# Attention and mixture feed-forward layer on 8 cores: slot waits kept across query halves, and the next head's operand copies issued one head earlier

## The chip, the cores and the metric

The program runs on all 8 cores of one Trainium2 chip. Every core works on two of the 16 sequences, with the same instructions, and no core talks to another. The metric is the device time of the slowest core in microseconds. The clock that is spoken of below is the one that TensorE (PE) was granted in a stretch, as a share of 2.4 GHz: 1.00 is 2.4 GHz and 0.50 is 1.2 GHz.

## What is computed

`x` is 16 x 2048 x 1024. After a layer norm the layer computes an attention with two steps, in which the output of step 0 is the query of step 1, and a feed-forward network with low-rank experts, of which each token uses two. Their product is added to `x`. The part around the change is the loop over steps:

```python
q = _l2norm(q)
k = _l2norm(k)
state = q
for _ in range(STEPS):                      # STEPS = 2
    sim = jnp.einsum('bqhd,bkhd->bqhk', state, k)
    att = jax.nn.softmax(BETA * sim, axis=-1)
    state = jnp.einsum('bqhk,bkhd->bqhd', att, v)
o = state.reshape(B, S, H) @ Wo + bo        # 16 heads of 64, S = 2048
...
x = x + s * silu(ffn(xn))
```

## The kernel before

Each core runs its two sequences one after the other. For each: norm and transposes; the projections to q, k and v (kept in SBUF as `qbuf`, `kbuf`, `vbuf`, bf16); the attention loop; the output projection; the feed-forward network over two halves of the tokens. A fence of all engines stands between these stages.

**The order of work is written out by hand.** A helper, `Prog.op`, appends an instruction to its engine's stream, in program order, with waits on counters: `tc_` counts TensorE instructions that release something, `vc` VectorE (DVE), `sc` ScalarE (ACT). A wait such as `(sc, sc.v)` is for the value that the counter has been brought to at the moment of writing, so it is for everything that was written before it on that engine. Every DVE and ACT instruction also waits for the one before it on its own engine. Each engine works through its stream in order.

**The attention loop** runs over 2 steps, 16 heads (`hh`) and 2 halves of the queries (`qh`, 1024 queries each). One pass through the inner body is called a half here. There are 64 halves per sequence, 128 per core. In a half, the 2048 keys are worked through in 16 chunks `c` of 128:

- `emit_sim(c)` (L613): two matmuls of 128x512 write the similarities of chunk `c` to half `c % 2` of `psb`. The first waits for the head's operands (`head_in`) and for the slot of `psb` (`sim_rel`).
- L629: ACT takes the exponential of 128x1024 from `psb` to the buffer `att[c % 4]` ("exp" below).
- L635: two matmuls add `v` times that into `psa`, over all 16 chunks. The first of a half also waits for `acc_gate`.
- `emit_sim` runs two chunks ahead of L635. At the start of a half chunks 0 and 1 are written first.

**The end of a half**: DVE copies the sum out of `psa` (L646, 65 rows, the last of them the softmax denominator), and ACT makes the reciprocal of that row by Ln (L649) and Exp (L652).

**The boundary between two heads** has two more parts. `head_copies(hh, step)` prepares the operands of a head in `kaugs[z]` and `staugs[z]`, with `z = hh % 2`: two DVE copies (L549, L552). In step 1 it also does ACT Square (L555), four pairs of a matmul (L559) and an ACT Ln (L563), an ACT Exp of the whole row (L567) and a DVE scaling (L569). `flush_tail` normalises the head before last: four times a pair of a 1-row fp32 matmul (two PE instructions, L586) and a DVE copy (L591), each waiting for the other, and after every second pair a DVE multiply into `qbuf` (L594). Its matmuls wait for `vc` at the value of the moment of writing.

So at the end of head `hh` the order of writing is: L646, L649, L652 of its second half, `head_copies(hh + 1)`, `flush_tail(hh - 1)`, and then the first half of head `hh + 1`. At the end of head 0 there is no tail to flush. After head 15 the last two tails are flushed.

At the start of each half, before, the lists of releases are written anew: `sim_rel` and `att_rel` with the values that `sc` and `tc_` have at that moment, `acc_gate` with that of `vc`. The last value of `sc` written by then is that of L652 (or of L567 after it), and that of `vc` belongs to L646, to L569 or to the last L594.

Of the kernel before, what the change touches and what calls it, by code (L numbers as in the profile page):

```python
# [18 lines left out]
NHEAD = 16  # L19
# [131 lines left out]
def build_program(S=2048, NB=2, dedup=True):  # L151
# [72 lines left out]
    tc_ = p.ctr("tc")  # L224
    vc = p.ctr("vc")
    sc = p.ctr("sc")
# [30 lines left out]
    def SC(fn, waits=(), inc=None, incn=1):  # L257
        p.op("scalar", fn, waits, inc, incn)
# [27 lines left out]
    for b in range(NB):  # L286
# [16 lines left out]
        for i in range(n_tt):  # L303
            sl = i % 2
            Y(lambda e, sl=sl, i=i, b=b: e.dma_start(out=xt[sl], in_=x_h[b, 128 * i:128 * (i + 1), :]),
              waits=[xrel[sl]], inc=xld[sl], incn=16)
            ldw = (xld[sl], xld[sl].v)
            SC(lambda e, sl=sl: e.activation(sqf, xt[sl], AF.Square),
               waits=[ldw, (vc, vc.v)], inc=sc)
            V(lambda e, sl=sl, i=i: e.reduce_sum(statc[:, i:i + 1], xt[sl], axis=AX.X),  # L310
              waits=[ldw], inc=vc)
            V(lambda e, i=i: e.reduce_sum(statc[:, 16 + i:17 + i], sqf, axis=AX.X),
              waits=[(sc, sc.v)], inc=vc)
# [30 lines left out]
        for i in range(n_tt):  # L344
            sl = i % 2
            Y(lambda e, sl=sl, i=i, b=b: e.dma_start(out=xt[sl], in_=x_h[b, 128 * i:128 * (i + 1), :]),
              waits=[xrelA[sl]], inc=xld[sl], incn=16)
# [3 lines left out]
              waits=[ldw, stats_done, (tc_, tc_.v)], inc=vc)  # L351
# [60 lines left out]
        for i in range(n_tt):  # L412
# [3 lines left out]
          waits=[(tc_, tc_.v)], inc=vc)  # L416
# [155 lines left out]
            return (vc, vc.v)  # L572

        tail_rel = [(vc, 0)]
        for step in range(2):
            heads_ready = [None] * (NHEAD + 1)
            heads_ready[0] = head_copies(0, step)
# [21 lines left out]
            for hh in range(NHEAD):  # L599
                z = hh % 2  # L600
                kaug = kaugs[z]
                stin = staugs[z]
                head_in = heads_ready[hh]
                for qh in range(NQH):
                    qco = HL * qh
                    sim_rel = [[(sc, sc.v)], [(sc, sc.v)]]
                    att_rel = [[(tc_, tc_.v)] for _ in range(4)]
                    acc_gate = [(vc, vc.v)]

                    def emit_sim(c):  # L610
                        sb = c % 2
                        for j2 in range(HL // 512):
                            T(lambda e, c=c, sb=sb, j2=j2, qco=qco, stin=stin, kaug=kaug: e.matmul(  # L613
                                psb[:, 1024 * sb + 512 * j2:1024 * sb + 512 * (j2 + 1)],
                                kaug[0:128, 128 * c:128 * (c + 1)],
                                stin[0:128, qco + 512 * j2:qco + 512 * (j2 + 1)],
                                start=True, stop=True),
                              waits=([head_in] + sim_rel[sb]) if j2 == 0 else [],
                              inc=(tc_ if j2 == HL // 512 - 1 else None))
                        return tc_.v  # L620

                    simv = [0] * n_tt
                    simv[0] = emit_sim(0)
                    if n_tt > 1:
                        simv[1] = emit_sim(1)
                    for c in range(n_tt):
                        sb = c % 2
                        ab = c % 4
                        SC(lambda e, ab=ab, sb=sb: e.activation(att[ab], psb[:, 1024 * sb:1024 * sb + HL],  # L629
                                                                AF.Exp),  # L630
                           waits=[(tc_, simv[c])] + att_rel[ab], inc=sc)
                        scv = sc.v
                        sim_rel[sb] = [(sc, scv)]
                        for j2 in range(HL // 512):
                            T(lambda e, c=c, ab=ab, j2=j2, hh=hh: e.matmul(  # L635
                                psa[0:128, 512 * j2:512 * (j2 + 1)],
                                vbuf[:, 1040 * c + 65 * hh:1040 * c + 65 * hh + 128],
                                att[ab][:, 512 * j2:512 * (j2 + 1)],
                                start=(c == 0), stop=(c == n_tt - 1)),
                              waits=([(sc, scv)] + (acc_gate if c == 0 else [])) if j2 == 0 else [],  # L640
                              inc=(tc_ if (c == n_tt - 1 and j2 == HL // 512 - 1) else None))
                        att_rel[ab] = [(tc_, tc_.v)]
                        if c + 2 < n_tt:
                            simv[c + 2] = emit_sim(c + 2)
                    st_ready = tc_.v
                    V(lambda e, z=z, qco=qco: e.tensor_copy(  # L646
                        stg[z][:, qco:qco + HL], psa[0:65, 0:HL]),
                      waits=[(tc_, st_ready)])
                    SC(lambda e, z=z, qco=qco: e.activation(  # L649
                        stg[z][64:65, qco:qco + HL], stg[z][64:65, qco:qco + HL], AF.Ln),  # L650
                       waits=[(vc, vc.v), (tc_, tc_.v)], inc=sc)
                    SC(lambda e, z=z, qco=qco: e.activation(  # L652
                        stg[z][64:65, qco:qco + HL], stg[z][64:65, qco:qco + HL],
                        AF.Exp, scale=-1.0), inc=sc)
                stg_v = (vc.v, sc.v)
                heads_ready[hh + 1] = head_copies(hh + 1, step) if hh + 1 < NHEAD else None
                if pending_tail is not None:
                    flush_tail(pending_tail)
                pending_tail = (hh, z, stg_v)
# [431 lines left out]
```

How the kernel before makes its waits and increments, by code:

```python
        def run(engine, _w=wlist, _inc=inc, _incn=incn, _fn=fn, _eng=eng):  # L68
            seen = self._waited[_eng]
            for c, v in _w:
                if self.dedup and seen.get(c.name, 0) >= v:
                    continue
                engine.wait_ge(c.sem, v)
                seen[c.name] = v
            inst = _fn(engine)
            if _inc is not None:
                inst.then_inc(_inc.sem, _incn)
            return inst
```

## Time and profile before

| | us |
|---|---|
| median of 2 runs | 12471.17 |
| lowest, highest | 12468.47, 12473.87 |
| the profiled execution | 12428.32 |
| its span, slowest core (core 6) | 12426.8 |
| spans of the eight cores | 12349.3 to 12426.8 |

The rows below come from the slowest core of the profiled execution. Times are microseconds from its first instruction. In a timeline a row is a run of like instructions of an engine: start, time it takes, engine, line, operation, tiles and count, and in brackets how long the engine had been idle before it and which instruction ended that.

### The profile page before, as it was taken

What the parts mean: (1) busy time and instruction counts of PE and PEld (TensorE: products, weight loads), DVE (VectorE), ACT (ScalarE), POOL (GpSimd) and SP (SyncE); (2) the same over time, 40 slices, a digit from 0 to 9 for tenths busy, and PEclk for the clock granted to TensorE, in tenths of its full rate; (3) what the DMA queues carried; (4) which work ended last, traced back from release to release, by engine and by line L of the source; (5) the groups of instructions that cost most, each with busy time, mean ns of one, the idle gap of its engine ahead of it and who ended that gap; (6) DMA issues with size and microseconds to landing.
All of it is one profiled execution on the core that took longest, in us unless ns stands there. A gap on an engine that the chain in (4) does not pass through costs nothing.

```text
span 12426.8 us, 89949 instructions; the slowest of 8 cores (12349.3 to 12426.8 us)
## 1 busy us (share of the span) xinstructions
PE 8045.1 (65%) x28266; PEld 2834.9 (23%) x28800; DVE 3310.3 (27%) x5351; ACT 3262.3 (26%) x3764; POOL 70.7 (1%) x137
## 2 busy tenths in 40 slices
PE   3566776666557773777446667766664687738775
PEld 2221111111123331333122211111111233313331
DVE  5222111111133332333352221111111333323333
ACT  1114665655200000000011146565661000000000
POOL 0000000000000000000000000000000000000000
PEclk6667887777778885889656678877777788858886
DMA  3100000000211102111120000000002011011111
GB/s 88 23 8 1 0 1 0 0 0 0 59 32 25 28 18 59 25 28 29 56 86 8 8 0 0 1 0 0 0 0 79 12 29 23 18 59 23 29 23 47
DMA packets 77408, 287.73 MB, mean 23 GB/s; under 512 B 8826, under 2 KB 17172, under 8 KB 66708
## 3 DMA queue, kind: packets, MB, share of 16 engines
q0 software_dynamic: 19040, 130.84, 5.6%
q1 hardware_dynamic: 57908, 151.10, 3.7%
q8 instruction: 246, 4.03, 0.1%
q14 instruction: 214, 1.75, 0.0%
HBM read 354.03 MB, written 58.72 MB: 33 GB/s over the span
## 4 chain that ended last, share of the span: by engine, by line
PE 49%; ACT 20%; DVE 17%; issue 8%; DMA 4%; SPq 1%; DVEq 1%; ACTq 1%; POOLq 0%
ACT arena L629 15%; PE psa L852 7%; PE psb L852 7%; PE psa L905 6%; PE psb L905 4%; PE psa L586 4%; PE psa L635 2%; PE psb L613 2%; DMA arena<-x 2%; PE psb L887 2%; PE psa L486 1%; DVE arena L876 1%; DVE arena L895 1%; DVE arena L591 1%; DVE arena L920 1%
## 5 line engine op out<-in xcount | busy, mean ns | idle before, releaser
L629 ACT ACTIVATE arena<-psb 128x1024 bf16<-128x1024 f32 x2048 | 2095.1, 1023 | 1291.7 <-PE psb L613 1041.0
L635 PE MATMUL psa<-arena 128*128 128x512 bf16 x4032 | 1296.7, 403 | 417.7 <-ACT arena L629 182.5
L613 PE MATMUL psb<-arena 128*128 128x512 bf16 x3986 | 1348.7, 428 | 325.5 <-ACT arena L652 254.5
L852 PE MATMUL psa<-arena 128*128 128x512 bf16 x4012 | 989.2, 388 | 131.6 <-DVE arena L920 111.7
L852 PE MATMUL psb<-arena 128*128 128x512 bf16 x4012 | 986.5, 387 | 4.7
L871 ACT ACTIVATE arena<-psa 128x512 f32<-128x512 f32 x256 | 152.8, 597 | 3155.6 <-PE psa L859 3143.6
L646 DVE COPY arena<-psa 65x1024 f32<-65x1024 f32 x128 | 156.3, 1221 | 2812.3 <-PE psa L635 2812.3
L905 PE MATMUL psa<-arena 128*128 128x512 bf16 x2008 | 741.7, 546 | 128.8 <-DVE arena L895 122.6
L586 PE MATMUL psa<-arena,onescf 1*64 1x512 f32 x512 | 484.3, 1046 | 467.0 <-DVE arena L594 153.5
L613 PEld LDWEIGHTS psb<-arena 128*128 128x128 bf16 x4096 | 419.5, 105 | 1001.2 <-issue 627.9
L905 PE MATMUL psb<-arena 128*128 128x512 bf16 x2008 | 534.7, 423 | 125.2 <-DVE arena L895 122.4
L635 PEld LDWEIGHTS psa<-arena 128*128 128x128 bf16 x4096 | 290.1, 100 | 1422.7 <-issue 1419.2
L852 PEld LDWEIGHTS psa<-arena 128*128 128x128 bf16 x4096 | 398.0, 99 | 662.1 <-issue 278.2
L887 PE MATMUL psb<-arena 128*128 128x512 bf16 x504 | 183.5, 450 | 527.2 <-DVE arena L881 404.2
L852 PEld LDWEIGHTS psb<-arena 128*128 128x128 bf16 x4096 | 407.1, 99 | 504.4 <-issue 90.4
L876 DVE TENSOR_TENSOR arena<-psa,arena 128x512 f32<-128x512 f32 x256 | 177.1, 692 | 1083.8 <-PE psa L859 1070.6
L920 DVE TENSOR_TENSOR arena<-psa,arena 128x512 f32<-128x512 f32 x480 | 332.1, 692 | 485.2 <-PE psa L905 484.8
L920 DVE TENSOR_TENSOR arena<-psb,arena 128x512 f32<-128x512 f32 x480 | 332.1, 692 | 289.8 <-PE psb L905 289.4
L905 PEld LDWEIGHTS psa<-arena 128*128 128x128 bf16 x2048 | 261.3, 132 | 639.2 <-issue 600.0
L871 ACT ACTIVATE arena<-psb 128x512 f32<-128x512 f32 x256 | 152.8, 597 | 867.8 <-PE psb L859 855.8
L876 DVE TENSOR_TENSOR arena<-psb,arena 128x512 f32<-128x512 f32 x256 | 177.1, 692 | 668.8 <-PE psb L859 655.5
L990 PE MATMUL psb<-idents,arena 128*128 128x128 f32 x256 | 114.4, 447 | 360.2 <-DVE arena L993 249.1
(165 smaller groups left out, 6276.9 us busy)
## 6 DMA issues: line engine op xcount, KB each, us to landing
arena<-wfs POOLq DMA_DIRECT2D x64, 1728.0 KB, 11.7
arena<-x SPq DMA_DIRECT2D x96, 512.0 KB, 3.7
xnsp<-arena SPq DMA_DIRECT2D x64, 256.0 KB, 3.9
arena<-xnsp SPq DMA_DIRECT2D x16, 1024.0 KB, 7.1
ssp<-arena SPq DMA_DIRECT2D x64, 256.0 KB, 2.6
arena<-ssp SPq DMA_DIRECT2D x32, 512.0 KB, 4.5
out<-arena SPq DMA_DIRECT2D x32, 512.0 KB, 2.9
nxsp<-arena SPq DMA_DIRECT2D x64, 128.0 KB, 4.3
```

What stands on the lines that cost most here:

```text
L486: T(lambda e, c=c, qsl=qsl, cols=cols, sl=sl: e.matmul(bankA(qsl), wsl[0][sl][:, 128 * c:128 * (c + 1)], x2T[:, S * c + cols.start:S * c + ...
L586: T(lambda e, z2=z2, qco2=qco2, j2=j2: e.matmul(psa[0:64, 1024:1536], onescf[64:65, :], stg[z2][64:65, qco2 + 512 * j2:qco2 + 512 * (j2 + 1)],
L613: T(lambda e, c=c, sb=sb, j2=j2, qco=qco, stin=stin, kaug=kaug: e.matmul(psb[:, 1024 * sb + 512 * j2:1024 * sb + 512 * (j2 + 1)], kaug[0:1 ...
L629: SC(lambda e, ab=ab, sb=sb: e.activation(att[ab], psb[:, 1024 * sb:1024 * sb + HL], AF.Exp), waits=[(tc_, simv[c])] + att_rel[ab], inc=sc)
L635: T(lambda e, c=c, ab=ab, j2=j2, hh=hh: e.matmul(psa[0:128, 512 * j2:512 * (j2 + 1)], vbuf[:, 1040 * c + 65 * hh:1040 * c + 65 * hh + 128] ...
L646: V(lambda e, z=z, qco=qco: e.tensor_copy(stg[z][:, qco:qco + HL], psa[0:65, 0:HL]), waits=[(tc_, st_ready)])
L852: wslb=wslb, tco=tco: e.matmul(grp(bank_i), wslb[:, FC * c + 128 * m:FC * c + 128 * (m + 1)], nxh[:, TH * c + tco:TH * c + tco + TC], star ...
L871: SC(lambda e, bi=bi, grp=grp: e.activation(silu_s[:, 512 * bi:512 * (bi + 1)], grp(bi), AF.Silu), waits=[(tc_, h1v), (vc, vc.v)], inc=sc)
L876: V(lambda e, bi=bi, grp=grp, j=j, tco=tco: e.tensor_tensor(h3w_s[:, 512 * bi:512 * (bi + 1)], grp(KC + bi), wexp[j][:, tco:tco + TC], ALU ...
L887: T(lambda e, c4=c4, j=j, rbank=rbank, sl=sl: e.matmul(rbank, a2sl[sl][:, 128 * c4:128 * (c4 + 1)], act2w[j][:, TC * c4:TC * (c4 + 1)], st ...
L905: sl=sl: e.matmul(grp(dd4), wsl2[sl][:, D * c4 + 128 * dd:D * c4 + 128 * (dd + 1)], act2w[j][:, TC * c4:TC * (c4 + 1)], start=(j == 0 and ...
L920: V(lambda e, dd=dd, dd4=dd4, grp=grp, tco=tco, wv=wv: e.tensor_tensor(outb[:, TH * dd + tco:TH * dd + tco + TC], grp(dd4), outb[:, TH * d ...
```

## The change

Two things are moved, and no instruction is added or taken away.

1. `sim_rel`, `att_rel` and `acc_gate` are set once ahead of both steps and then carried from half to half. The first similarities of a half wait for the exps that read the two slots of `psb` last, and no longer for L652. The first L635 of a half waits, for `psa`, for the L646 before it, and no longer for the last DVE instruction written.
2. `head_copies(hh + 1)` is written at the start of head `hh` rather than at its end. At a boundary between heads the order of writing is now: L646, L649, L652 of head `hh`, `flush_tail(hh - 1)`, `head_copies(hh + 2)`, first half of head `hh + 1`. Ahead of head 0 of each step stand `head_copies(0)` and `head_copies(1)`, and at the boundary from head 14 to 15 there are no copies.

```diff
         tail_rel = [(vc, 0)]
+        sim_rel = [[(sc, sc.v)], [(sc, sc.v)]]
+        att_rel = [[(tc_, tc_.v)] for _ in range(4)]
+        acc_gate = [[(vc, vc.v)]]
         for step in range(2):
...
                 head_in = heads_ready[hh]
+                if hh + 1 < NHEAD:
+                    heads_ready[hh + 1] = head_copies(hh + 1, step)
                 for qh in range(NQH):
                     qco = HL * qh
-                    sim_rel = [[(sc, sc.v)], [(sc, sc.v)]]
-                    att_rel = [[(tc_, tc_.v)] for _ in range(4)]
-                    acc_gate = [(vc, vc.v)]
...
-                              waits=([(sc, scv)] + (acc_gate if c == 0 else [])) if j2 == 0 else [],
+                              waits=([(sc, scv)] + (acc_gate[0] if c == 0 else [])) if j2 == 0 else [],
...
                       waits=[(tc_, st_ready)])
+                    acc_gate[0] = [(vc, vc.v)]
...
                 stg_v = (vc.v, sc.v)
-                heads_ready[hh + 1] = head_copies(hh + 1, step) if hh + 1 < NHEAD else None
                 if pending_tail is not None:
                     flush_tail(pending_tail)
```

## Rows read from the trace of the kernel before

**Rows 1.** The page: the chain that ended last, by line, and the costliest group.
```profile
ACT arena L629 15%; PE psa L852 7%; PE psb L852 7%; PE psa L905 6%; PE psb L905 4%; PE psa L586 4%; PE psa L635 2%; PE psb L613 2%; DMA arena<-x 2%; PE psb L887 2%; PE psa L486 1%; DVE arena L876 1%; DVE arena L895 1%; DVE arena L591 1%; DVE arena L920 1%
...
L629 ACT ACTIVATE arena<-psb 128x1024 bf16<-128x1024 f32 x2048 | 2095.1, 1023 | 1291.7 <-PE psb L613 1041.0
```

**Rows 2.** Windows: steps 0 and 1, first sequence; last three columns: clock, DMA share, GB/s.
```profile
1088.00:2060.00 972.00, 692.04 (x2125) 193.19 (x2168) 136.17 (x153) 591.11 (x576) 0.00 (x0) 0.82 0.00 0
2060.00:3245.00 1185.00, 747.45 (x2202) 201.41 (x2246) 158.98 (x181) 689.67 (x672) 0.00 (x0) 0.76 0.00 0
```

**Rows 3.** Timeline, ACT: from the first half to the second of head 0.
```profile
1098.47 11.55 ACT L629 ACTIVATE arena<-psb 128x1024 bf16<-128x1024 f32 x10
...
1113.38 1.05 ACT L652 ACTIVATE arena<-arena 1x1024 f32<-1x1024 f32 x1
1115.68 2.19 ACT L629 ACTIVATE arena<-psb 128x1024 bf16<-128x1024 f32 x2 [1.25 <-PE psb L613]
```

**Rows 4.** Timeline, PE: the same boundary.
```profile
1110.16 0.59 PE L635 MATMUL psa<-arena 128*128 128x512 bf16 x2 [0.58 <-ACT arena L629]
1114.57 1.86 PE L613 MATMUL psb<-arena 128*128 128x512 bf16 x4 [3.82 <-ACT arena L652]
1116.95 1.01 PE L635 MATMUL psa<-arena 128*128 128x512 bf16 x2 [0.52 <-ACT arena L629]
```

**Rows 5.** Windows over the same boundary; PE's clock is the third number from the end.
```profile
1110.00:1115.00 5.00, 1.02 (x4) 0.31 (x5) 1.22 (x1) 2.12 (x3) 0.00 (x0) 0.75 0.00 0
1115.00:1120.00 5.00, 4.47 (x12) 1.22 (x10) 0.00 (x0) 3.07 (x3) 0.00 (x0) 0.57 0.00 0
```

**Rows 6.** Timeline, step 0, boundary from head 1 to head 2.
```profile
1186.66 1.22 DVE L646 COPY arena<-psa 65x1024 f32<-65x1024 f32 x1 [24.42 <-PE psa L635]
...
1189.61 1.93 PE L586 MATMUL psa<-arena,onescf 1*64 1x512 f32 x2 [3.05 <-DVE arena L552]
...
1199.54 1.94 PE L586 MATMUL psa<-arena,onescf 1*64 1x512 f32 x2 [0.94 <-DVE arena L591]
...
1201.40 1.89 PE L613 MATMUL psb<-arena 128*128 128x512 bf16 x4
...
1202.53 2.19 ACT L629 ACTIVATE arena<-psb 128x1024 bf16<-128x1024 f32 x2 [12.31 <-PE psb L613]
```

**Rows 7.** Timeline, step 0, first matmul pair of the tail one head later.
```profile
1252.01 1.54 PE L586 MATMUL psa<-arena,onescf 1*64 1x512 f32 x2 [3.06 <-DVE arena L552]
```

**Rows 8.** Timeline, step 1, boundary from head 1 to head 2.
```profile
2196.61 1.22 DVE L646 COPY arena<-psa 65x1024 f32<-65x1024 f32 x1 [24.44 <-PE psa L635]
...
2200.32 1.91 ACT L555 ACTIVATE arena<-arena 64x2048 bf16<-64x2048 bf16 x1
...
2207.95 1.91 ACT L567 ACTIVATE arena<-arena 1x2048 bf16<-1x2048 bf16 x1
2209.96 0.69 DVE L569 TENSOR_SCALAR arena<-arena 1x2048 bf16<-1x2048 bf16 x1 [10.55 <-ACT arena L567]
2210.79 1.93 PE L586 MATMUL psa<-arena,onescf 1*64 1x512 f32 x2 [3.62 <-DVE arena L569]
...
2222.59 1.89 PE L613 MATMUL psb<-arena 128*128 128x512 bf16 x4
...
2223.55 1.22 DVE L594 TENSOR_TENSOR arena<-arena 64x1024 bf16<-64x1024 f32 x1
2223.72 2.19 ACT L629 ACTIVATE arena<-psb 128x1024 bf16<-128x1024 f32 x2 [13.86 <-PE psb L613]
...
2226.95 1.02 ACT L629 ACTIVATE arena<-psb 128x1024 bf16<-128x1024 f32 x1 [1.04 <-PE psb L613]
...
2228.66 15.06 ACT L629 ACTIVATE arena<-psb 128x1024 bf16<-128x1024 f32 x13 [0.68 <-PE psb L613]
```

**Rows 9.** Timeline, PE, end of step 1: a tail that waits for L646 alone.
```profile
3221.93 1.94 PE L586 MATMUL psa<-arena,onescf 1*64 1x512 f32 x2 [1.47 <-DVE arena L646]
```

**Rows 10.** Timeline, ACT, step 1: first exps of head 1, where no tail is flushed.
```profile
2150.83 2.19 ACT L629 ACTIVATE arena<-psb 128x1024 bf16<-128x1024 f32 x2 [2.15 <-PE psb L613]
```

## The prediction

> **What bounds the kernel now.** I read the page's chain first, then the costliest groups, then the windows by stage, then the timeline of each kind of boundary between halves. The chain names the exp (L629) as its largest line, 15%, and the group row gives 2048 of them at 1.023 us [rows 1]. The change touches only the attention loop: 972 us for step 0 and 1185 us for step 1 of one sequence, twice that per core, about 4314 of 12427 us. ACT is busy 591 and 690 us of these [rows 2], so a good third of the loop is time in which the exps stand still. Inside a half they don't: 10 exps take 11.55 us [rows 3], 1.17 us each, and PE fits its four matmuls under that. What stands still is the boundary between halves, and the change moves nothing else. So the argument is about when the first exp of the next half starts, and in what clock PE is then.
>
> There are five kinds of boundary. Lags come from the same rows: 0.10 us from one ACT instruction to the next, 0.15 us from DVE to PE or from DVE to ACT, and 0.25 us from an exp to PE at the half clock (1115.68 + 1.02 = 1116.70, L635 at 1116.95) [rows 3, 4].
>
> **A. Half to half inside a head: 64 per core, and 2 more in step 0 from head 0 to head 1, where there is no tail.** Before, the last exp ends at 1098.47 + 11.55 = 1110.02. L646, Ln and Exp follow, the Exp ends at 1114.43, and only then PE may start the similarities, at 1114.57, so the exp starts at 1115.68 [rows 3, 4]. With the change PE starts them right after the last L635 of the half, which ends at 1110.75 [rows 4]. ACT still works in order: Ln and Exp stay ahead of the exp, as they were. So the exp starts at 1114.43 + 0.10 = 1114.53, and 1.15 us are saved. 66 x 1.15 = 75.9 us. The rest of the 5.66 us gap stays, because L646, Ln and Exp are as they were.
>
> **B. Head to head in step 0, with a tail: 28 per core (14 in each of two).** Before, L646 ends at 1187.88, the two copies follow, and the tail's first matmul starts at 1189.61 [rows 6]. With the change it waits for L646 alone. At the end of the step it does that already: it starts 0.15 us after (the idle of 1.47 us there is the 0.10 us to L646, its 1.22 us, and 0.15 us) [rows 9]. So it starts at 1188.03, 1.58 us earlier, and the tail, the similarities and the exp behind it move with it: 28 x 1.58 = 44.2 us. The 1.58 us is also what the two copies take with their lags. They now stand behind the tail on DVE, under the exps, where nothing waits for DVE for 24 us [rows 6]. I cost them at nothing. Without this cover the 1.58 us would come back.
>
> **C. Head to head in step 1, with a tail and copies: 26 (heads 1 to 13).** Here both parts are long. Before: L646 ends at 2197.83; Square starts at 2200.32 and the chain of Square, matmuls, Lns and Exp ends at 2209.86 (9.54 us); L569; the tail from 2210.79, its matmuls to 2222.6; similarities; exp at 2223.72 [rows 8]. The change swaps them and leaves them in series, since the copies of head `hh + 2` stand behind the tail on DVE and in front of the similarities on PE and of the exps on ACT. After: 2197.83 + 0.15, then the tail through to the end of its last L594 (2210.79 to 2224.77, 13.98 us), then the copies 1.58, lag 0.15, the chain 9.54, lag 0.10: exp at 2223.33. That is only 0.39 us earlier. What is gained (Ln and Exp of the denominator, L569 and the similarities are hidden) is nearly paid back, as the last L591, L594 and the copies are no longer hidden. 26 x 0.39 = 10.1 us.
>
> **D. Step 1, head 14 to 15: 2.** No copies are left. The tail starts at 2197.98 and the exp 12.93 us after its start (2210.79 to 2223.72) [rows 8], at 2210.91: 12.81 us each, 25.6 us.
>
> **E. Step 1, head 0 to 1: 2.** No tail. The exp stands 2.15 us behind L567 now [rows 10] and will stand 0.10 us behind it: 2 x 2.05 = 4.1 us.
>
> **F. Start of step 1: 2.** The copies of head 1 and their chain stand ahead of head 0's similarities. Before, the exp starts 2.15 - 0.10 - 0.69 = 1.36 us after L569 [rows 8, 10]. After, it is 1.58 + 0.15 + 9.54 + 0.10 = 11.37 us. A loss of 2 x 10.0 = 20.0 us. In step 0 the same copies are 1.58 us on DVE, beside the first similarities, and nobody waits.
>
> Sum of A to F: 75.9 + 44.2 + 10.1 + 25.6 + 4.1 - 20.0 = 139.9 us.
>
> **G. What the clock takes back.** Around an A boundary PE falls to 1.2 GHz: the clock is 0.75 in the one stretch and 0.57 in the next [rows 5]. At 1.2 GHz a round of four matmuls takes 1.71 us (2226.95 to 2228.66) [rows 8] instead of 1.17 us, so each slow round costs 0.54 us of exp time. Before, PE comes back with the similarities, 1.11 us ahead of the first exp. After, those are done by about 1111.7 (half of 1.86 us for four, behind 1110.75), and PE comes back with L635, 1.02 + 0.25 = 1.27 us behind the first exp. Its gap grows from 3.82 to about 4.1 us, and its recovery starts 2.4 us later seen from the exps. If the slow stretch after the restart is as long as now, that costs 2.4 x 0.54 / 1.71 = 0.75 us. That is the upper bound. The lower bound is nothing, where the extra matmuls at the front of the gap make the clock fall later by as much. I see no row that decides, and take 0.35, about the middle. It holds in A, C, E and F (66 + 26 + 2 + 2 = 96), where the exp now comes after an idle PE: -33.6 us. In B and D PE runs from the tail straight into similarities and exps as before.
>
> The Trainium skill ("TensorE: Matmul & The Clock Gate", the section on the HAM clock gate) says that half rate is the default and that activity releases it, and its section on oscillation warns of loops whose gaps throttle PE each time round. This speaks against the change, which shortens no idle stretch of PE. By it the upper bound holds, and the time would be 12403 us with H at nothing. With G at nothing, and H as below, it would be 12312 us.
>
> **H. What the clock gives.** The tail's first pair takes 1.93 us at the half clock, 1.54 us where it still caught the full one [rows 6, 7]. In step 1 it stands 15 us behind the last exp and is always slow [rows 8]. It now comes 1.58 us earlier in step 0 and 12.8 us earlier in step 1, so it will catch the full clock more often. Bounds: nothing, and 0.9 us (both matmuls of the pair at about half of 1.93). I take 0.35 for 56 boundaries: 19.6 us.
>
> Total: 139.9 - 33.6 + 19.6 = 125.9 us. The profiled execution took 12428.3 us, the median of the runs 12471.2, 0.34% more. The sum is of boundaries whose lengths do not depend on that, so I take it off the median: 12345 us, 1.0% less. Measurement can tell about 2% from no change, so this counts as the same.
>
> **Rivals.**
> 1. *The clock takes nearly everything back.* G at 0.75 for 96 boundaries is 72 us, H nothing: 68 us are left, 12403 us. For it: PE idles longer than before at 66 boundaries. Against: PE does 0.9 us more work at the front of the gap.
> 2. *PE no longer falls to 1.2 GHz inside a head.* Then the third exp doesn't wait 1.04 us, nor the fourth 0.68 (0.10 to 0.15 us of each is the usual lag) [rows 8]. That is 0.9 to 1.4 us more at 66 boundaries, some 75 us, with G gone there: 12471 - 140 - 20 - 75 + 11 = 12247 us. Against: the gap is as long as the one that makes it fall now.
> 3. *A does nothing,* because the first exp was never held by the similarities but by something else that stays. Then B to F, H and the smaller part of G are left: 64 + 20 - 10 = 74 us, 12397 us. Against: the row names L613 as what ended 1.25 us of idle.
> 4. *Slower: PE stays at 1.2 GHz far into each half.* The place is the restart after an A or C boundary. The price is 0.54 us for every further slow round. The saving of about 160 us (A to F and H) is used up at 1.7 us over 96 boundaries, about 3 slow rounds more than now. If all of the 13 rounds that now run fast were slow, an A boundary would cost 7 us and the kernel would take 12471 + 66 x 7 - 160 = 12773 us. Against: at 1.2 GHz PE is never idle in these rounds, and in today's trace the clock then comes back after two or three of them [rows 5, 8].
>
> **How the numbers follow.** The forecast has 0.62, rival 1 0.16, rival 2 0.10, rival 3 0.06, rival 4 0.03, and 0.03 are for what I don't see. The likeliest one's own ends are G at 0.75 with H at nothing (12403) and G at nothing with H at 0.9 (12281). Executions of one kernel differ by some 0.3% (12428 and 12471 here), which I add in part: 12265 to 12430. This holds rivals 1 and 3 and leaves out rivals 2 and 4. Faster by over 2% needs 249 us, more than rival 2 gives: 0.03. Slower by over 2% is rival 4 in its full form: 0.02. Within 2%: 0.95.
>
> **What the profile would show.** A: four L613 right behind the last L635 of a half, and a gap between exps of 4.5 us for 5.66. B: L586 0.15 us after L646. C: L586 ahead of L555, L549 behind the last L594, and a gap nearly as before. D: one gap of about 15 us where the others of step 1 have 27. F: two chains of L555 to L567 ahead of step 1. G: the exps' wait for L613 at the third to fifth exp of a half, which would grow from 1041 us less the first exp's 1.25 at each A boundary. I am wrong if PE's mean clock in the loop leaves 0.76 to 0.82 by much, or if the boundaries of C change by more than 1 us.

## The result and the profile after

The changed kernel takes 12371.4 us (median of 15 runs, 12230 to 12470) against 12484.8 us before (14 runs, 12393 to 12671). Some executions of either kernel run slower, with a lower clock on one die, and the ratio is taken without them: 0.9903, with a 95% interval of 0.9857 to 0.9949. That is 0.97% less, or 121 us of 12485, somewhere between 64 and 179. By the bound of 2% it is the same. Forecast were 126 us less and 12345 us.

The total is a blunt measure, so what follows reads the attention loop by itself: from the first exp of step 0 to the last exp of step 1, for both sequences, as a mean over the eight cores of the profiled execution. It fell from 4264.3 to 4131.5 us, by 132.8 us. The changed kernel profiled a second time gave 4128.1.

The page after. The first row is the chain by line, the others are groups: count, busy us and mean ns, then idle time before them and what ended most of it.

```profile
ACT arena L631 15%; PE psa L854 8%; PE psb L854 7%; PE psa L907 6%; PE psb L907 4%; PE psa L589 4%; PE psa L637 3%; PE psb L615 2%; DMA arena<-x 2%; PE psa L486 2%; PE psb L889 1%; DVE arena L878 1%; DVE arena L897 1%; DVE arena L922 1%; DVE arena L883 1%
...
L631 ACT ACTIVATE arena<-psb 128x1024 bf16<-128x1024 f32 x2048 | 2097.5, 1024 | 823.3 <-PE psb L615 575.0
L637 PE MATMUL psa<-arena 128*128 128x512 bf16 x4096 | 1352.7, 414 | 682.6 <-ACT arena L631 483.8
L615 PE MATMUL psb<-arena 128*128 128x512 bf16 x4096 | 1368.9, 425 | 43.0 <-DVE arena L552 43.0
```

The exp is L631 now, the similarities L615, the sum over the keys L637. The exps waited 1041 us for the similarities before [rows 1] and wait 575 us now. Yet the loop is only 133 us shorter. On the slowest core, 863 us of the 1041 stood before the first exp of a half and 178 us before the others; now it is 341 and 234. Most of the first exp's wait has moved to another name: Ln, Exp of the denominator (kind A), or the chain from Square to Exp (kind C), still stand ahead of it in ACT's order and hold it back.

**A, a boundary inside a head.** ACT's timeline (start, duration, line, count, idle and what ended it), to be held beside rows 3:

```profile
1099.61 10.39 ACT L631 ACTIVATE arena<-psb 128x1024 bf16<-128x1024 f32 x9
...
1113.36 1.05 ACT L655 ACTIVATE arena<-arena 1x1024 f32<-1x1024 f32 x1
1114.56 2.20 ACT L631 ACTIVATE arena<-psb 128x1024 bf16<-128x1024 f32 x2
1117.79 1.02 ACT L631 ACTIVATE arena<-psb 128x1024 bf16<-128x1024 f32 x1 [1.04 <-PE psb L615]
1119.50 1.02 ACT L631 ACTIVATE arena<-psb 128x1024 bf16<-128x1024 f32 x1 [0.68 <-PE psb L615]
1121.20 4.54 ACT L631 ACTIVATE arena<-psb 128x1024 bf16<-128x1024 f32 x4 [0.68 <-PE psb L615]
```

PE over the same boundary, beside rows 4, and the windows (the clock is the third number from the end), beside rows 5:

```profile
1110.58 1.03 PE L615 MATMUL psb<-arena 128*128 128x512 bf16 x4
1115.83 1.01 PE L637 MATMUL psa<-arena 128*128 128x512 bf16 x2 [4.23 <-ACT arena L631]
```

```profile
1110.00:1115.00 5.00, 1.46 (x6) 0.52 (x6) 1.22 (x1) 2.55 (x4) 0.00 (x0) 0.91 0.00 0
1115.00:1120.00 5.00, 4.17 (x10) 1.41 (x11) 0.00 (x0) 3.13 (x4) 0.00 (x0) 0.50 0.00 0
1120.00:1125.00 5.00, 4.30 (x17) 1.42 (x16) 0.00 (x0) 3.88 (x5) 0.00 (x0) 0.90 0.00 0
```

The four similarities run at the full clock behind the last L637, in 1.03 us for 1.86. The first exp starts right behind L655, with no idle in brackets. But PE then stands still for 4.23 us (3.82 before), comes back at 1.2 GHz with L637, and the third, fourth and fifth exps wait for it.

**B, between heads in step 0**, beside rows 6. The tail's matmuls are L589:

```profile
1184.98 1.22 DVE L648 COPY arena<-psa 65x1024 f32<-65x1024 f32 x1 [23.27 <-PE psa L637]
1186.35 1.04 PE L589 MATMUL psa<-arena,onescf 1*64 1x512 f32 x2 [1.47 <-DVE arena L648]
...
1188.32 1.04 PE L589 MATMUL psa<-arena,onescf 1*64 1x512 f32 x2 [0.94 <-DVE arena L594]
...
1194.49 1.93 PE L589 MATMUL psa<-arena,onescf 1*64 1x512 f32 x2 [0.94 <-DVE arena L594]
1196.36 1.89 PE L615 MATMUL psb<-arena 128*128 128x512 bf16 x4
```

The tail starts 0.15 us behind the copy out of `psa` instead of 1.73 us. It also reaches PE while the clock is still full: its first two pairs take 1.04 us each, where the pair of rows 6 took 1.93.

**C, between heads in step 1**, beside rows 8:

```profile
2165.70 1.93 PE L589 MATMUL psa<-arena,onescf 1*64 1x512 f32 x2 [1.47 <-DVE arena L648]
...
2178.45 1.22 DVE L597 TENSOR_TENSOR arena<-arena 64x1024 bf16<-64x1024 f32 x1
2179.77 0.69 DVE L549 COPY arena<-arena 64x2048 bf16<-64x2048 bf16 x1
...
2181.40 1.91 ACT L555 ACTIVATE arena<-arena 64x2048 bf16<-64x2048 bf16 x1 [13.50 <-DVE arena L552]
...
2191.08 2.19 ACT L631 ACTIVATE arena<-psb 128x1024 bf16<-128x1024 f32 x2
```

Tail, copies, chain and exp stand in series: 25.38 us from the first L589 to the exp, where the terms of C add up to 25.35.

The kinds of boundary, worked out from the timelines of all eight cores: mean gap from the last exp of a half to the first of the next, and mean length of the half that follows this gap (first to last exp), all in us. Sixteen exps back to back take 18.6 us.

| kind, count | gap, kernel before | gap, changed | half, kernel before | half, changed | saved in all, us |
|---|---|---|---|---|---|
| A, 66 | 5.61 | 4.57 | 19.78 | 20.12 | 46.0 |
| B, 28 | 16.48 | 14.24 | 19.78 | 19.81 | 62.0 |
| C, 26 | 28.01 | 26.97 | 19.79 | 20.18 | 16.9 |
| D, 2 | 27.95 | 14.35 | 19.88 | 19.81 | 27.4 |
| E, 2 | 16.25 | 14.24 | 19.60 | 20.45 | 2.3 |
| F, 2 | 42.70 | 52.95 | 19.56 | 20.07 | -21.5 |

They add up to 133.1 us, for the 132.8 us measured from end to end.

### The profile page after: what moved, and what is told of

The parts are those of the page before. It is cut to its first block, busy times and chain, and to the rows that moved or that the text cites. A ratio compares the mean times of both kernels' runs of the same rounds, so it can differ in the third digit from the quotient of the medians.

```text
span 12346.9 us, 90329 instructions; the slowest of 8 cores (12222.2 to 12346.9 us)
## 1 busy us (share of the span) xinstructions
PE 8112.2 (66%) x28800; PEld 2855.0 (23%) x28800; DVE 3310.4 (27%) x5351; ACT 3265.1 (26%) x3764; POOL 70.7 (1%) x137
## 4 chain that ended last, share of the span: by engine, by line
PE 51%; ACT 20%; DVE 16%; issue 7%; DMA 4%; SPq 1%; DVEq 1%; ACTq 1%; POOLq 0%
ACT arena L631 15%; PE psa L854 8%; PE psb L854 7%; PE psa L907 6%; PE psb L907 4%; PE psa L589 4%; PE psa L637 3%; PE psb L615 2%; DMA arena<-x 2%; PE psa L486 2%; PE psb L889 1%; DVE arena L878 1%; DVE arena L897 1%; DVE arena L922 1%; DVE arena L883 1%
## 5 line engine op out<-in xcount | busy, mean ns | idle before, releaser
L631 ACT ACTIVATE arena<-psb 128x1024 bf16<-128x1024 f32 x2048 | 2097.5, 1024 | 823.3 <-PE psb L615 575.0
L637 PE MATMUL psa<-arena 128*128 128x512 bf16 x4096 | 1352.7, 414 | 682.6 <-ACT arena L631 483.8
L615 PE MATMUL psb<-arena 128*128 128x512 bf16 x4096 | 1368.9, 425 | 43.0 <-DVE arena L552 43.0
L854 PE MATMUL psa<-arena 128*128 128x512 bf16 x4096 | 1010.2, 391 | 126.0 <-DVE arena L922 111.1
L854 PE MATMUL psb<-arena 128*128 128x512 bf16 x4096 | 1007.6, 391 | 0.0
L648 DVE COPY arena<-psa 65x1024 f32<-65x1024 f32 x128 | 156.3, 1221 | 2742.2 <-PE psa L637 2742.2
L907 PE MATMUL psa<-arena 128*128 128x512 bf16 x2048 | 741.8, 542 | 121.3 <-DVE arena L897 121.3
L637 PEld LDWEIGHTS psa<-arena 128*128 128x128 bf16 x4096 | 300.9, 101 | 1686.1 <-issue 1683.0
L589 PE MATMUL psa<-arena,onescf 1*64 1x512 f32 x512 | 445.0, 965 | 362.0 <-DVE arena L597 153.5
L907 PE MATMUL psb<-arena 128*128 128x512 bf16 x2048 | 551.1, 431 | 121.3 <-DVE arena L897 121.3
L615 PEld LDWEIGHTS psb<-arena 128*128 128x128 bf16 x4096 | 428.4, 106 | 698.1 <-issue 315.9
L854 PEld LDWEIGHTS psa<-arena 128*128 128x128 bf16 x4096 | 401.1, 100 | 671.6 <-issue 318.0
L854 PEld LDWEIGHTS psb<-arena 128*128 128x128 bf16 x4096 | 409.8, 100 | 513.2 <-issue 128.0
L889 PE MATMUL psb<-arena 128*128 128x512 bf16 x512 | 177.8, 432 | 525.4 <-DVE arena L883 403.3
```

Of the source, the lines that this page charges most:

```text
L589: T(lambda e, z2=z2, qco2=qco2, j2=j2: e.matmul(psa[0:64, 1024:1536], onescf[64:65, :], stg[z2][64:65, qco2 + 512 * j2:qco2 + 512 * (j2 + 1)],
L637: T(lambda e, c=c, ab=ab, j2=j2, hh=hh: e.matmul(psa[0:128, 512 * j2:512 * (j2 + 1)], vbuf[:, 1040 * c + 65 * hh:1040 * c + 65 * hh + 128] ...
L648: V(lambda e, z=z, qco=qco: e.tensor_copy(stg[z][:, qco:qco + HL], psa[0:65, 0:HL]), waits=[(tc_, st_ready)])
L854: wslb=wslb, tco=tco: e.matmul(grp(bank_i), wslb[:, FC * c + 128 * m:FC * c + 128 * (m + 1)], nxh[:, TH * c + tco:TH * c + tco + TC], star ...
L889: T(lambda e, c4=c4, j=j, rbank=rbank, sl=sl: e.matmul(rbank, a2sl[sl][:, 128 * c4:128 * (c4 + 1)], act2w[j][:, TC * c4:TC * (c4 + 1)], st ...
L907: sl=sl: e.matmul(grp(dd4), wsl2[sl][:, D * c4 + 128 * dd:D * c4 + 128 * (dd + 1)], act2w[j][:, TC * c4:TC * (c4 + 1)], start=(j == 0 and ...
```

## Experiments

Each is a whole kernel, profiled once, and read by the same means over eight cores. "Loop" is the attention loop as above: 4264.3 us before, 4131.5 us changed. The first five were timed only once or twice, with totals between 12286 and 12584 us. The kernel before spreads as widely (12370 to 12671 us), so their totals decide nothing and only the loop is read. Each diff says against which kernel it is; "..." marks lines left out.

### Part 1 alone

Against the changed kernel:

```diff
                 head_in = heads_ready[hh]
-                if hh + 1 < NHEAD:
-                    heads_ready[hh + 1] = head_copies(hh + 1, step)
...
                 stg_v = (vc.v, sc.v)
+                heads_ready[hh + 1] = head_copies(hh + 1, step) if hh + 1 < NHEAD else None
```

> Part 1 of the change alone: the three wait lists are carried from half to half, and the copies of the next head stand at the end of a head, as before. My theory: only A is won. The gap between exps inside a head falls from about 5.62 us (mean before) to 4.56 as in the changed kernel, and the half behind it is some 0.3 us longer. The gaps between heads stay: about 16.4 us in step 0 (mean), 28.0 in step 1 with the 14-to-15 boundary among them, 16.2 for step 1's head 0 to 1, and step 1 starts 43 us behind step 0. Attention is shorter than before by 66 x (1.06 - 0.33) = 48 us over both sequences, from 4171 us (first to last exp of each of the four steps) to about 4123. Rival: the similarities in front matter little by themselves and most of the 131 us came through the boundaries between heads; then the gap inside a head stays near 5.6 and attention hardly moves.

Measured: the gap inside a head is 4.57 us, and all gaps between heads stay (16.7, 28.0, 16.1, and 42.8 at the start of step 1). So the early similarities do shorten this gap, and there the rival falls. Its other half holds: of the 133 us in the table, 46 come from A and 87 from the boundaries between heads. And the halves behind A grew by 0.65 us instead of 0.33, to 20.4 us, and the loop is 4235.1 us: 29 us saved, not 48. In these halves PE spends 5.6 us at 1.2 GHz, 3.9 us before and 4.3 us in the changed kernel. PE restarts 1.3 us behind the first exp in this kernel and in the changed one alike, so where the clock turns is not a matter of this boundary alone. I can't say what fixes it.

### Part 2 alone

Against the kernel before:

```diff
                 head_in = heads_ready[hh]
+                if hh + 1 < NHEAD:
+                    heads_ready[hh + 1] = head_copies(hh + 1, step)
                 for qh in range(NQH):
...
                 stg_v = (vc.v, sc.v)
-                heads_ready[hh + 1] = head_copies(hh + 1, step) if hh + 1 < NHEAD else None
```

> Part 2 alone: the copies of the next head are written at the start of a head, and the wait lists are written anew at each half, as before. My theory: the gap inside a head stays 5.6 us. In step 0 between heads the tail starts 1.6 us earlier and the gap falls to about 14.1 us, but the first L635 of the half now waits for every DVE instruction written so far, so for the last L594 and both copies behind it: it comes about 3.2 us behind the first exp's start for 1.27, and most of the gain is given back inside the half (halves behind these boundaries about 1.5 us longer). In step 1 the similarities wait for L567, so the gap with tail and copies is about 28.2 us, the 14-to-15 one about 14.2, the start of step 1 about 54 us. In sum about 20 us are won on 4214 us (the four steps and the two gaps between steps), far less than 131 less 48: the parts would not add up, because part 1 takes away the waits that part 2 makes dear. Rival: the parts are independent, then this kernel wins about 131 - 48 = 83 us.

Measured: 4247.5 us, 17 us saved. Parts 1 and 2 by themselves give 29 + 17 = 46 us, and together 133. The first half of a head shows why. PE and DVE behind a tail in step 0:

```profile
1198.34 1.89 PE L615 MATMUL psb<-arena 128*128 128x512 bf16 x4
1202.60 1.01 PE L637 MATMUL psa<-arena 128*128 128x512 bf16 x2 [2.38 <-DVE arena L552]
```

```profile
1199.65 1.22 DVE L594 TENSOR_TENSOR arena<-arena 64x1024 bf16<-64x1024 f32 x1 [0.46 <-DVE arena L591]
1200.97 0.69 DVE L549 COPY arena<-arena 64x2048 bf16<-64x2048 bf16 x1
1201.77 0.69 DVE L552 COPY arena<-arena 64x2048 bf16<-64x2048 bf16 x1
```

The tail starts early and the gap is 13.9 us. But the wait for `psa` is for everything written on DVE so far, and that now includes the copies for a head that starts one whole head later. The half is 22.0 us long for 19.8. At the boundary from head 14 to 15, where no copies stand, it is 19.9 in the same kernel.

### Part 2 with one of the three lists

Against the changed kernel, which keeps `acc_gate` carried:

```diff
-        sim_rel = [[(sc, sc.v)], [(sc, sc.v)]]
-        att_rel = [[(tc_, tc_.v)] for _ in range(4)]
         acc_gate = [[(vc, vc.v)]]
...
                 for qh in range(NQH):
                     qco = HL * qh
+                    sim_rel = [[(sc, sc.v)], [(sc, sc.v)]]
+                    att_rel = [[(tc_, tc_.v)] for _ in range(4)]
```

> The copies alone (as in e2_copies_only) with one of the three wait lists carried, acc_gate: the first L635 of a half waits for the last copy out of psa alone, while the similarities still wait for all ACT instructions written so far. My theory: in e2 the halves behind a boundary of step 0 were 22.0 us long for 19.8, because this L635 waited 2.38 us for the next head's copies behind the tail. With this one wait gone they fall back to about 20 us, the gaps in front of them stay at about 14 us, the gap inside a head stays 5.6 us, and the loop falls from 4247 us to 4247 - 28 x 2 = about 4190 us. Rival: the similarities' wait is what holds these halves; then they stay at 22 us and the loop at 4247 us.

Measured: 4192.0 us, expected about 4190. The halves behind B are 19.6 us, the gap in front of them 14.6, the gap inside a head still 5.6. So one wait made 55 us of difference: the one that the copies had been moved in front of. The rest, 60 us to 4131.5, comes with the other two lists, which let the similarities start early.

### Early copies in step 0 only

Against the changed kernel:

```diff
-                if hh + 1 < NHEAD:
+                if hh + 1 < NHEAD and step == 0:
                     heads_ready[hh + 1] = head_copies(hh + 1, step)
...
                 stg_v = (vc.v, sc.v)
+                if hh + 1 < NHEAD and step == 1:
+                    heads_ready[hh + 1] = head_copies(hh + 1, step)
```

> The changed kernel with the copies of step 1 back at the end of a head (step 0 keeps them early). My theory, from the terms C to F: gaps of step 1 go back to 28.0 us (26 of them, and 2 at head 14 to 15), 16.2 at head 0 to 1, and the start of step 1 from 53 to 43 us. Against the changed kernel that costs 26 x (1.03 less 0.47 of longer halves) + 2 x 13.7 + 2 x 0.9 and gives back 2 x 9.6 + 2 x 0.9 at the start: about 22 us more over 4 steps and 2 step gaps. Rival: in step 1 the move is worth nothing or harms, since the copies are in series with the tail either way; then the sum is equal to the changed kernel's or below it.

Measured: the gaps of step 1 went back as expected (28.0, 28.0, 16.2, start 43.0). The loop is 4176.8 us, 45 us more than the changed kernel and not 22. Gap and half together, C costs 13 us (47.66 for 47.15, 26 times), D 27 and E 2, and F gives 21 back (62.7 for 73.0, twice): 21 us for the four kinds that were changed, as expected. B adds 6 us, and A another 18, with gap and half 0.17 to 0.38 us longer, though nothing was changed there. The early copies of step 1 are worth some 21 us by themselves. In the halves behind A, PE spends 5.0 us at 1.2 GHz for 4.3, so these 18 us go with the clock, again at places that the edit doesn't touch. Behind B it is 4.3 us in both kernels, and where the 6 us come from stays open.

### PE kept busy at the boundary inside a head

Against the changed kernel:

```diff
+NFILL = 12
...
                         simv[1] = emit_sim(1)
+                    if qh == 1:
+                        for _ in range(NFILL):
+                            T(lambda e, stin=stin, kaug=kaug: e.matmul(
+                                psa[:, 1536:2048], kaug[0:128, 0:128], stin[0:128, 0:512],
+                                start=True, stop=True))
```

> The changed kernel with 12 more matmuls of 128x512 on PE at each boundary inside a head, behind the early similarities, into a bank of PSUM that nobody reads (64 per core; extra work whose results are dropped, the output is unchanged). They fill about 2.6 us of the 4.1 us in which PE would stand still. My theory: what makes the halves behind these boundaries 20.1 us long, where 16 exps back to back are 18.6, is PE's 1.2 GHz after the gap. With the filling PE stays at 2.4 GHz, the gap stays 4.56 us, and the halves fall to about 18.8 us: 64 x 1.3 = 83 us less attention than in the changed kernel. Rival: the halves are long for another reason, an order of waits at their start; then they stay at 20.1 us, and if PE is at 1.2 GHz in the gap anyway the filler takes 12 x 0.43 = 5.1 us and pushes the first L637 back by about 1 us, to halves of 21 us.

Measured: the gap stays 4.58 us, and the halves behind it are 18.83 us, for 20.12. The loop is 4067.1 us, 64 us less than the changed kernel (expected 83; the gaps of B were 0.6 us longer). Twelve useless matmuls make the kernel faster. PE and the windows at such a boundary:

```profile
1113.33 2.75 PE L631 MATMUL psa<-arena 128*128 128x512 bf16 x12
...
1117.73 0.59 PE L643 MATMUL psa<-arena 128*128 128x512 bf16 x2 [1.65 <-ACT arena L637]
1118.16 0.59 PE L616 MATMUL psb<-arena 128*128 128x512 bf16 x2
```

```profile
1110.00:1115.00 5.00, 4.27 (x20) 1.63 (x19) 1.22 (x1) 2.64 (x3) 0.00 (x0) 1.00 0.00 0
1115.00:1120.00 5.00, 3.13 (x14) 0.94 (x12) 0.00 (x0) 4.29 (x5) 0.00 (x0) 1.00 0.00 0
```

The clock is 1.00 throughout. Over all eight cores these halves have 0.01 us at 1.2 GHz on average, for 4.3. This shows term G to be the clock: it costs 1.3 us per half in the changed kernel. Held against the same 18.83 us, it cost about 1.0 before; the filling was not tried in that kernel.

### Ln and Exp of the denominator behind the next two exps

Against the changed kernel. `recip` holds the Ln and the Exp:

```diff
                         sim_rel[sb] = [(sc, scv)]
+                        if c == 1 and later[0] is not None:
+                            later[0]()
+                            later[0] = None
...
+                    if qh == 0:
+                        later[0] = recip
+                    else:
+                        recip()
```

> The changed kernel, with the Ln and Exp of the denominator of each head's first half moved behind the first two exps of the second half on ACT (64 places). My theory: with the early similarities the next exp is held by nothing but the place of Ln and Exp in ACT's order. So at a boundary inside a head the first exp starts about 1.4 us after the last one (similarities behind the last L635 and the lags) for 4.57 us, and 2.3 us for Ln and Exp stand between the second and third exp. PE is never idle for more than about 2 us, stays at 2.4 GHz, and the third to fifth exp don't wait. Gap plus half falls from 24.7 us to 1.4 + 18.7 + 2.3 = 22.4 us, 64 times: 147 us less than the changed kernel in the loop, from 4131 to about 3985 us, and about 12371 - 147 = 12225 us in all. Rival: the clock falls anyway, since PE's work at the boundary is thin in either order; then gap plus half is about 23.8 us and the loop about 4075 us.

Measured: 12237.0 us, ratio to the kernel before 0.9776 (0.9607 to 0.9945), which leaves open whether it is over or under 2%. The loop is 4014.2 us, 117 us less than the changed kernel, and the gap 1.27 us. This settles what holds the first exp in the changed kernel: Ln and Exp in front of it. Gap and half together take 22.95 us, between my 22.4 and the rival's 23.8. The expectation that PE would stay at 2.4 GHz was wrong:

```profile
1114.22 1.05 ACT L660 ACTIVATE arena<-arena 1x1024 f32<-1x1024 f32 x1
1115.42 2.19 ACT L632 ACTIVATE arena<-psb 128x1024 bf16<-128x1024 f32 x2
1116.59 0.59 PE L641 MATMUL psa<-arena 128*128 128x512 bf16 x2 [2.49 <-ACT arena L632]
1117.02 1.02 PE L616 MATMUL psb<-arena 128*128 128x512 bf16 x2
```

Behind a gap of only 2.49 us the clock fell. It did so in 59% of these halves, for 2.0 us of a half on average.

### All boundaries taken apart

All chunks of a step form one sequence. Here `u` is the number of the chunk within its head, 0 to 31. Ln and Exp, the pieces of the tail and the pieces of the copies are put between its chunks. Against the changed kernel, in part:

```diff
+            for t in range(2 * n_tt * NHEAD):
+                hh, qh, c = t // (2 * n_tt), (t // n_tt) % 2, t % n_tt
...
+                if c == 2 and cp_v[0] is not None:
+                    recip(*cp_v[0])
+                    cp_v[0] = None
+                if hh + 1 < NHEAD:
+                    if qh == 0 and c == 4:
+                        copies(hh + 1)
+                    if step == 1:
...
+                        if u == 8:
+                            square(hh + 1)
+                        if u in (12, 15, 20, 23):
+                            norm_mm((12, 15, 20, 23).index(u))
...
+                    if u in (6, 10, 18, 22):
+                        k = (6, 10, 18, 22).index(u)
+                        tail_pair(hh - 1, k // 2, k % 2)
```

> A version built on what the boundaries showed: all 512 chunks of a step run as one sequence, the similarities two chunks ahead also over the boundary of halves and heads; the Ln and Exp of a half stand behind the third exp of the next; the tail of the head before and the copies of the head after (with the chain of Square, matmuls, Lns and Exp in step 1) are spread in single pieces over the chunks of a head. The same instructions, other order and waits. My theory: ACT is then never held by more than its own work. Per head in step 0 it has 32 x 1.17 + 4 x 1.15 = 42 us against 59 in the changed kernel, in step 1 7 us more, 49 against 72. With the start and end of each step: 2 x 16 x (17 + 23) = 1280 us at most, about 1100 us less after what PE's tail matmuls (0.6 us each, more than PE's slack in a round of 0.3 us) take back, so the loop falls from 4131 to about 3050 us and the kernel from 12371 to about 11270 us. Rival 1: PE becomes the bound, since its work per round grows and stands at 0.81 of the clock once it is dense on all cores of a die: rounds of 1.3 us for 1.17 would give back 2048 x 0.13 = 270 us, about 11540 us. Rival 2: the loop's time was not set by these boundaries, and little changes.

Measured: 11465.2 us, ratio to the kernel before 0.9157 (0.8997 to 0.9317). The loop is 3276.5 us, 855 us less than in the changed kernel. The gaps are 0.15 to 0.16 us at every boundary of every kind but F, the start of step 1, where 25.8 us stay. What was missed to 3050 us is mostly in the halves: 22.7 to 23.0 us in step 0 for 21 expected, 26.6 to 28.8 us in step 1 for 24.5. The kernel moves many pieces at once, and what each of them is worth was not tried. ACT around one pair of Ln and Exp:

```profile
1211.39 1.05 ACT L632 ACTIVATE arena<-arena 1x1024 f32<-1x1024 f32 x1
1212.54 1.05 ACT L635 ACTIVATE arena<-arena 1x1024 f32<-1x1024 f32 x1
1213.74 2.20 ACT L688 ACTIVATE arena<-psb 128x1024 bf16<-128x1024 f32 x2
1216.61 1.03 ACT L688 ACTIVATE arena<-psb 128x1024 bf16<-128x1024 f32 x1 [0.67 <-PE psb L673]
1218.32 3.37 ACT L688 ACTIVATE arena<-psb 128x1024 bf16<-128x1024 f32 x3 [0.68 <-PE psb L673]
```

The exps wait 0.67 and 0.68 us soon after it, as behind the A boundaries. That led to the last kernel.

### The same with Ln and Exp apart

Against the kernel just shown. `recip` keeps the Ln, `recip2` has the Exp:

```diff
+        def recip2(hh, qh, v):
...
                 if c == 2 and cp_v[0] is not None:
                     recip(*cp_v[0])
+                if c == 4 and cp_v[0] is not None:
+                    recip2(*cp_v[0])
                     cp_v[0] = None
```

> The version of e6_pipelined with one piece moved: the Exp of the denominator stands two chunks behind its Ln, so that ACT leaves PE without exps for 1.15 us twice instead of for 2.3 us once. In e6 59% of the halves in the middle of a head still had a stretch at 1.2 GHz, 2.2 us on average, and the exps waited 344 us for the similarities on its slowest core. My theory: it is the 2.3 us in a row that lets the clock fall. Split, PE stays at 2.4 GHz (or 0.81 of it), these halves have hardly a slow stretch, each half is 0.6 to 1 us shorter, and the loop falls from 3276 to about 3200 us. Rival: the clock falls because of the single-row matmuls of the tail and of the norm, which count little; then the slow stretches and the loop stay as in e6.

Measured: 11377.4 us, ratio to the kernel before 0.9090 (0.8985 to 0.9195). The loop is 3204.5 us, expected 3200. In step 0 no half behind a boundary has a stretch at 1.2 GHz any more, on any core, neither inside a head nor between heads. Only the first half of each sequence, which follows no other half, has one (3.3 us). In step 1 the halves inside a head have 1.6 us of it for 1.3, and those at the start of a head 4.6 us for 7.5. From head 1 on, the tail's single-row matmuls are in the halves of step 0 too, so they are not what lets the clock fall there. In step 1 the clock still falls, and the matmuls of the norm stand there alone; for these the rival stays open.

```profile
1118.95 1.05 ACT L632 ACTIVATE arena<-arena 1x1024 f32<-1x1024 f32 x1
1120.15 2.19 ACT L691 ACTIVATE arena<-psb 128x1024 bf16<-128x1024 f32 x2
1122.43 1.05 ACT L638 ACTIVATE arena<-arena 1x1024 f32<-1x1024 f32 x1
1123.63 16.25 ACT L691 ACTIVATE arena<-psb 128x1024 bf16<-128x1024 f32 x14
```

This is the fastest version, 9% below the kernel before and 8% below the changed one. Its loop is 927 us shorter than the changed kernel's.

### The changed kernel once more

> The changed kernel once more, unaltered, to see how far the numbers of one profile repeat. Expected: each mean gap within 0.3 us of the first profile, the halves within 0.3 us (their slow stretch depends on where the clock changes), the loop at 4131 us within 15 us, and most of the spread between executions (12230 to 12470 us) outside the attention loop. If the loop itself moves by some 50 us, the differences read between single profiles above are not to be trusted.

Measured: the loop is 4128.1 us (4131.5 the first time), every mean gap within 0.3 us, every mean half within 0.2. But this execution took 12517 us for 12349, from spans of 12515 and 12347 us. The difference lies outside the loop: on that core, 119 us of the 168 in the stages behind the loop of the first sequence and 47 us in those behind the second. In the feed-forward stage of the same core, first the earlier profile, then this one (clock: third number from the end):

```profile
3430.00:6200.00 2770.00, 1906.45 (x7359) 748.74 (x7359) 969.77 (x1480) 193.19 (x305) 15.83 (x30) 0.82 0.14 33
```

```profile
3430.00:6200.00 2770.00, 2023.12 (x7295) 768.62 (x7295) 911.74 (x1374) 175.87 (x286) 15.82 (x30) 0.77 0.12 27
```

## Why the prediction was right

The total came out as forecast, 121 us (64 to 179) for 126, and the loop, which can be read more sharply, at 133. Step by step:

- **A.** Forecast 1.15 us per gap, measured 1.04. One part is the lag behind an ACT instruction, 0.15 us here and not 0.10. The other is that I took 5.66 us for every gap before, where the mean is 5.61 (the gaps ran from 5.24 to 5.76). 66 gaps gave 69 us for 76. Rival 3, that something else holds the exp, is out: the first exp now stands right behind L655, and it moves when Ln and Exp are moved.
- **B.** 1.58 us was right to the hundredth: L589 starts 0.15 us behind L648. Costing the moved copies at nothing held only because `acc_gate` went with them. The prediction named DVE's 24 us of idle as their cover, which was the lesser half of the answer. The runs showed the other half: without the carried wait L637 waits for them, 2.4 us, and the half behind grows by 2.2 us.
- **C, D, E, F.** In this order, 0.39, 12.81, 2.05 and -10.0 us forecast without the clock, 1.04, 13.60, 2.01 and -10.25 measured. The order in which tail, copies and chain would stand, and that C gains next to nothing, was as worked out. By the prediction's own sign of being wrong, a change of more than 1 us at C, the gap is just over it (1.04 us). Term H, which counts there as well, is the 0.65 us that lie between.
- **G.** Forecast +0.35 us for the halves behind A, C, E and F. Measured +0.34 at A, +0.39 at C, +0.85 at E and +0.51 at F. The middle of two bounds hit. It was a choice and not knowledge: part 1 alone gave +0.65, close to the upper bound of 0.75. Nor did the slow stretch stay as long behind the restart as the upper bound supposed. Over the eight cores it ran, at A, from 2.1 us ahead of the first exp to 3.9 us behind it, and now runs from 0.9 to 5.2 us behind it; from the restart on, it was 5.0 us and is 4.0 us. That the clock is the mechanism is shown by the filled boundary, where the whole of it goes away. The prediction's sign for G was not right as written: the exps' wait for the similarities did not grow from 1041 us less A's share but fell to 575, because in C and F the first exp no longer waits under that name and in B and D it waits less. The wait of the later exps, which G is about, grew from 178 to 234 us.
- **H.** This term was mis-sized. Forecast 0.35 us per tail, measured 0.66 at B (2.24 less 1.58), 0.65 at C and 0.79 at D. I had bounded it by one pair catching the full clock; in the trace two do. The pairs' own durations agree: at B the first pair fell from 1.68 to 1.33 us on average and the second from 1.93 to 1.64, at C from 1.93 to 1.50 and 1.71, and the last two stayed at 1.93. That gave 17 us more than forecast, and A's shorter gap took 7 back. PE's idle time before the tail is 1.47 us at B for 3.07, so the prediction's sentence that the change shortens no idle stretch of PE doesn't hold there.

The other rivals: rival 1, the clock taking nearly everything back, did not happen in the changed kernel. Part 1 alone came nearer to it: the shorter gaps at A gave 68 us, and the longer halves behind them took back 42. Rival 2, PE not falling at all, did not happen by itself, only with the filling. Rival 4, PE slow far into the half, did not happen: the slow stretch grew from 3.9 to 4.3 us.

The Trainium skill ("TensorE: Matmul & The Clock Gate", HAM oscillation) describes a loop in which the gap between two bursts of matmuls throttles PE each time round. The trace agrees: no half behind an A boundary was free of a slow stretch, before or after. What the change leaves at each of the 66 A boundaries is the larger part: a gap of 4.57 us, and the 1.3 us that the slow clock costs behind it.

## What to carry to other kernels

A wait written as "everything so far" gets dearer with every instruction that is moved in front of it. Before work is moved early, look for such waits behind its new place, and carry the exact release instead: each of the two parts here won 17 to 29 us alone, the moved work with the one wait behind it made exact won 72, and both parts together 133. And where the gap between two bursts of matmuls is set by short work on another engine, spread that work between the bursts' own steps. That won seven times as much, 927 us beyond the changed kernel, as the change had won over the kernel before.

## What the runs showed of the hardware

- With Ln and Exp moved behind the next two exps, PE's clock still fell in 59% of the halves behind a boundary inside a head, in the one shown behind a gap of 2.49 us. In step 0 it never fell behind a boundary where the two pieces of 1.05 us stood apart, with exps and matmuls between them. Where exactly it turns also moved with changes elsewhere in the loop: the slow stretch in the halves behind A was 3.9, 4.3, 5.0 and 5.6 us in four kernels. What sets it stays open.
- The traces show a third level, 0.81 of the clock, for a varying share of the time. On one core it lasted 880 us in one profile of the changed kernel, all of it behind the last attention loop, and 2451 us in the next, 2300 of them outside the loops. In the feed-forward windows above, the matmuls of L854 took 379 ns each in the first profile and 408 to 414 ns in the second. The two executions differ by 1.4%, more than the change itself is worth, and the loop by 3 us. That the level makes the difference was read from the two profiles and not tried by itself.
